# Four transformer layers on one core: expert weights by SyncE's direct DMAs, and GpSimd's scatters and fetches one by one behind a TensorE product

## The reference

```
x = x + xattn0(ln(x), ctx);  x = x + ln(x) @ sign(weight).T
x = x + xattn1(ln(x), ctx)
h = ln(x)                                   # 2048 tokens
score = softmax(h @ gate_w.T);  w, e = top_k(score, 2)
x = x + sum_k w_k * (silu(h @ w_gate[e_k]) * (h @ w_up[e_k])) @ w_down[e_k] + shared(h)
x = x + xattn2(ctx, ln(x), mask);  x = x + ternary_ffn(ln(x))
x = x + xattn3(ln(x), ctx);        x = x + three_lora_blocks(ln(x))
```

## Time and profile before

| | us |
|---|---|
| median of 3 runs (1206.04 to 1211.15) | 1206.27 |
| the profiled execution | 1206.1 |
| its span, first to last instruction | 1204.3 |
| TensorE busy | 1059.1 |
| VectorE busy | 935.3 |
| ScalarE busy | 825.4 |
| GpSimd busy | 549.8 |

### The profile page before, as it was taken

How to read it: one execution, slowest core, us unless ns; L and a number is a source line. 1 busy time by engine, 2 the same in 40 slices (tenths; PEclk the granted TensorE clock), 3 DMA queues, 4 the chain that set the end, 5 groups by cost and what they waited for, 6 DMA issues and landing times.

```text
span 1204.3 us, 25939 instructions
## 1 busy us (share of the span) xinstructions
PE 1059.1 (88%) x8349; PEld 787.6 (65%) x8406; DVE 935.3 (78%) x3207; ACT 825.4 (69%) x1560; POOL 549.8 (46%) x1089
## 2 busy tenths in 40 slices
PE   5899999987999988799899997689998999988876
PEld 4677777775878866567677774347575665656654
DVE  1888888777555679897777698899989989898633
ACT  4677756655665646557557767459989798998963
POOL 5233255665444466468744426124424432324235
PEclk8999999999999999999999999889999999999989
DMA  5675542325577542513387762132212222121000
GB/s 175 200 242 185 173 113 67 98 68 149 174 225 195 171 137 71 149 36 106 113 250 231 230 200 79 53 90 67 73 35 66 80 62 80 54 63 54 10 10 18
DMA packets 98356, 140.01 MB, mean 116 GB/s; under 512 B 12336, under 2 KB 79792, under 8 KB 98224
## 3 DMA queue, kind: packets, MB, share of 16 engines
q1 hardware_dynamic: 90192, 105.58, 29.7%
q0 software_dynamic: 8032, 32.78, 9.0%
HBM read 65.43 MB, written 22.54 MB: 73 GB/s over the span
## 4 chain that ended last, share of the span: by engine, by line
PE 47%; DVE 21%; ACT 12%; issue 9%; DMA 4%; POOL 3%; another core or an unknown queue 2%; SPq 1%; DVEq 0%; ACTq 0%; POOLq 0%
PE ps L1513 10%; PE ps L1634 5%; PE ps L1533 4%; PE ps L1551 4%; PE ps L1506 4%; PE ps L1726 4%; ACT probs L1942 3%; DVE neg_max L2197 3%; DVE ps L2193 3%; PE ps L1520 3%; PE ps L1733 2%; DVE bn L2074 2%; DMA w<-in_expert,w_row 2%; ACT q_st L1957 2%
## 5 line engine op out<-in xcount | busy, mean ns | idle before, releaser
L1942 ACT ACTIVATE probs<-ps 128x384 f32<-128x384 f32 (+1 forms) x512 | 264.0, 545 | 62.4 <-PE ps L1554 28.8
L1533 PE MATMUL ps<-k_st,q_st 96*128 96x256 bf16 (+1 forms) x1024 | 173.7, 261 | 26.0 <-DVE neg_max L2197 10.8
L1551 PE MATMUL ps<-q_st,k_st 104*128 104x256 bf16 (+1 forms) x1024 | 179.0, 261 | 14.8 <-ACT probs L1942 6.6
L2197 DVE TENSOR_REDUCE neg_max<-ps 128x2 f32<-128x512 f32 x256 | 168.2, 680 | 12.2 <-PE ps L1536 6.4
L1957 ACT ACTIVATE q_st<-ps 8x1024 bf16<-8x1024 f32 x128 | 130.2, 1017 | 48.9 <-PE ps L1616 39.0
L2193 DVE CUSTOM_DVE_ANT_0 ps<-ps,diag_s 128x128 f32<-128x128 f32 (+1 forms) x384 | 123.2, 358 | 30.9 <-PE ps L1533 21.9
L2514 POOL TENSOR_SCALAR var_eps<-mv 128x2 f32<-128x2 f32 (+1 forms) x115 | 27.5, 239 | 253.2 <-DVE mv L2077 242.3
L1533 PEld LDWEIGHTS ps<-k_st,q_st 96*128 96x128 bf16 x1024 | 86.6, 98 | 75.5 <-DVE neg_max L2197 21.2
L1551 PEld LDWEIGHTS ps<-q_st,k_st 104*128 104x128 bf16 x1024 | 89.8, 98 | 61.2 <-issue 17.9
L1634 PE MATMUL ps<-probs,v 128*32 128x256 f32 (+1 forms) x2048 | 125.4, 363 | 4.3 <-ACT probs L1942 2.6
L2532 POOL CAST parts<-qf 128x512 bf16<-128x512 f32 x64 | 39.8, 622 | 150.1 <-DVE qf L2099 67.9
(11 more groups left out here) (271 smaller groups left out, 2584.5 us busy)
## 6 DMA issues: line engine op xcount, KB each, us to landing
k_st<-parts SPq DMA_DIRECT2D x192, 128.0 KB
q_st<-parts SPq DMA_DIRECT2D x192, 128.0 KB
x_rows<-wo SPq DMA_DIRECT2D x10, 768.0 KB, 6.5
ctx_t<-in_ctx_t SPq DMA_DIRECT2D x16, 256.0 KB, 3.9
ring<-x_rows SPq DMA_DIRECT2D x31, 128.0 KB
y_rows<-ring SPq DMA_DIRECT2D x31, 128.0 KB
xn_t<-x_rows SPq DMA_DIRECT2D x31, 128.0 KB
y_rows<-vec SPq DMA_DIRECT2D x31, 128.0 KB
```

The lines of the kernel that those rows point to most:

```text
L1533: last = mm(t[:, c0:c0 + n], head(q_st, r, h, KROWS, j * P, P), head(k_st, r, h, KROWS, 0, n), start=j == 0 or L != 2, stop=L != 2, skip_g ...
L1551: last = mm(t[:, j * S:j * S + n], head(k_st, r, h, KALL, j * P, P), head(q_st, r, h, KALL, skip, n), start=j == 0 or L == 3, stop=L == 3, ...
L1942: nc.scalar.activation(probs[:, (hg % 2) * HPG + h4, 0:width], tile_of(key)[:, 0:width], ACT.Exp, scale=SCALE).then_inc(*tile_drained(key))
L2197: V.tensor_reduce(neg_max[:, hg, h4, :], tile_of(key).rearrange("p (j t) -> p j t", j=SJ), AX.X, ALU.max, negate=True).then_inc(*tile_drai ...
```

## The change

1. `gather` moves from GpSimd's stream to SyncE's. SyncE waits for the same semaphores, reads the expert's row number from `w_row` into a register, and issues one direct DMA from there.
2. `scatter` and `fetch` are cut into four steps each, one for each indirect DMA, with a time of its own in `AT`.
3. Ahead of each of these 64 DMAs GpSimd waits for the last score product of TensorE that the plan puts before the DMA (`wait_score`).
4. All of `AT` is written anew. Its last step stands at 1117.9 us, where it stood at 1120.5.

```diff
-    yield
-    part.scatter(b)
+    for a in range(SJ):
+        for k in range(TOP_K):
+            yield
+            part.scatter(b, a, k)
...
-    yield
-    part.fetch(b)
+    for a in range(SJ):
+        for k in range(TOP_K):
+            yield
+            part.fetch(b, a, k)
     yield
     part.merge(b)
...
+            def wait_score():
+
+                n = sum(10 * clock[0] > t for t in AT[0])
+                if n:
+                    L, b = ORDER[(n - 1) // H]
+                    wait_filled(pool, ("s", L, b, *divmod((n - 1) % H, HPG)))
...
-                def gather(i):
-                    wait_drained(pool, ("tile_e", i // GT))
-                    if i >= RING:
-                        wait_filled(pool, ("gd", i - RING))
-                    G.indirect_dma_start(expert[:, i % RING, :], None, expert_d,
-                                         bass.IndirectOffsetOnAxis(ap=w_row[:, i:i + 1], axis=0)).then_inc(*w_tile_in[i % RING].step(i))
...
+                    wait_score()
+                    G.indirect_dma_start(x_rows[b // NB], bass.IndirectOffsetOnAxis(ap=dest[:, b * SJ + a, k:k + 1], axis=0),
+                                         xn[:, NORMED["l1f"], a, :], None).then_inc(*scattered.step((b, a, k)))
...
+                    wait_score()
+                    G.indirect_dma_start(y_in(b, n), None, y_rows[g],
+                                         bass.IndirectOffsetOnAxis(ap=dest[:, T, k:k + 1], axis=0)).then_inc(*y_back[n % RING].step(n))
...
+                def gather(i):
+                    wait_drained(sp, ("tile_e", i // GT))
+                    if i >= RING:
+                        wait_filled(sp, ("gd", i - RING))
+                    row = sp.value_load(w_row[0:1, i:i + 1], min_val=0, max_val=(E - 1) * P)
+                    sp.dma_start(expert[:, i % RING, :], expert_d[bass.ds(row, P), :]).then_inc(*w_tile_in[i % RING].step(i))
```

More of the change, by code:

```diff
@@ L2661, in allotted, with scatter, fetch @@
                     done(G.tensor_tensor(owner[:, b // NB, :], owner[:, b // NB, :], less[:, 1, :], ALU.add), "owner")
-                def scatter(b):
-                    pool.wait_ge(*place.at(("dest", b)))
-                    pool.wait_ge(*ln_done.at(("l1f", b, SJ - 1)))
-                    if b == 0:
-                        pool.wait_ge(*filling.at(11))
-                    for a in range(SJ):
-                        for k in range(TOP_K):
-                            G.indirect_dma_start(x_rows[b // NB], bass.IndirectOffsetOnAxis(ap=dest[:, b * SJ + a, k:k + 1], axis=0),
-                                                 xn[:, NORMED["l1f"], a, :], None).then_inc(*scattered.step((b, a, k)))
-                def gather(i):
-                    wait_drained(pool, ("tile_e", i // GT))
-                    if i >= RING:
-                        wait_filled(pool, ("gd", i - RING))
-                    G.indirect_dma_start(expert[:, i % RING, :], None, expert_d,
-                                         bass.IndirectOffsetOnAxis(ap=w_row[:, i:i + 1], axis=0)).then_inc(*w_tile_in[i % RING].step(i))
-                def fetch(b):
-                    g = b // NB
-                    if b % NB == 0:
+                def scatter(b, a, k):
+                    if a == k == 0:
+                        pool.wait_ge(*place.at(("dest", b)))
+                        pool.wait_ge(*ln_done.at(("l1f", b, SJ - 1)))
+                        if b == 0:
+                            pool.wait_ge(*filling.at(11))
+                    wait_score()
+                    G.indirect_dma_start(x_rows[b // NB], bass.IndirectOffsetOnAxis(ap=dest[:, b * SJ + a, k:k + 1], axis=0),
+                                         xn[:, NORMED["l1f"], a, :], None).then_inc(*scattered.step((b, a, k)))
+                def fetch(b, a, k):
+                    g, T = b // NB, b * SJ + a
+                    n = T * TOP_K + k
+                    if b % NB:
+                        pool.wait_ge(*merged.at((b - 1, a, k)))
+                    elif a == k == 0:
                         wait_filled(pool, ("gt", (g + 1) * GT - 1))
@@ L2686, in fetch @@
                             pool.wait_ge(*y_out[i % RING].at(i))
-                    for a in range(SJ):
-                        for k in range(TOP_K):
-                            T = b * SJ + a
-                            n = T * TOP_K + k
-                            if b % NB:
-                                pool.wait_ge(*merged.at((b - 1, a, k)))
-                            G.indirect_dma_start(y_in(b, n), None, y_rows[g],
-                                                 bass.IndirectOffsetOnAxis(ap=dest[:, T, k:k + 1], axis=0)).then_inc(*y_back[n % RING].step(n))
+                    wait_score()
+                    G.indirect_dma_start(y_in(b, n), None, y_rows[g],
+                                         bass.IndirectOffsetOnAxis(ap=dest[:, T, k:k + 1], axis=0)).then_inc(*y_back[n % RING].step(n))
                 def block_power(n, b):
```

## The result

| | before, us | after, us | ratio |
|---|---|---|---|
| medians of 13 and 13 runs on one chip | 1208.83 | 1198.55 | 0.9906 [0.9885, 0.9927] |
| once more on another chip, 20 and 12 runs | 1207.64 | 1198.82 | 0.9928 [0.9901, 0.9955] |

What follows compares the result with a forecast made beforehand. No engine was full; TensorE's work (busy 88%) plus its waits was taken as the time. 1206.1 - 13 - 1.5 + 0 + 4 - 1.3 = 1194.3, 0.2 more by the median, taken as 1194 us; range 1177 to 1207.

Steps and rivals of the forecast that it cites:

- The reading of the stalls: During bursts of indirect DMAs on GpSimd, news of finished TensorE products reaches other engines only afterwards; 29 us of stalls.
- Rival 2: Stalls come from the transfers' own traffic or chance, not GpSimd, and stay; 1207.5 us, chance 0.07.
- Rival 1: Waits on GpSimd don't break the bursts; only what the gathers prolonged goes; 1202 us, chance 0.16.
- 1% or less: Predicted share of the changed kernel's chain under "another core or an unknown queue", 2% before.
- 1 us at most: Predicted longest joint restart delay of ScalarE and VectorE right behind a burst in the changed profile.
- -13 us for the stalls: At 16 bursts of scatters and fetches: 19 us of stall go, 0.7 of it counts, between -5 and -24.
- The added waits on GpSimd, 0: 64 waits for scores on GpSimd cost nothing, being hidden by slack; at worst 13.9 us.
- The slack that I named: GpSimd's 242.3 us in 58 waits, 4.2 us each, said to hide a wait of one or two us.
- GpSimd relieved, -1.5: 62 gathers leave GpSimd, so `power` and splits come sooner; a tenth of ScalarE's 13.9 us wait for `shift`.
- SyncE loaded, +4 us: Loads, stores and stacks queue behind gathers of 1.3 us each on SyncE; between 0 and 9 us.
- The new table, -1.3 ± 5: The rewritten order of steps ends 2.6 us earlier in the plan; half counted, ±5 us either way.
- Rivals 3 and 4: SyncE bounds the expert stretches, 1220 us, chance 0.10; all stalls count, single gathers hold signals too, 1178 us, chance 0.15.

Runs made afterwards that it cites:

- r_after: The changed kernel, unchanged, run again on chip C beside the kernel before: 1198.82 us, ratio 0.9928.
- e2: The changed kernel with its own table and split steps but without its waits for score products, on chip A: 1199.53 us, ratio 0.9933 to before.
- e9: The kernel before with split steps and waits ahead of scatters, fetches and also gathers, gathers on GpSimd, on chip B: 1194.05 us, ratio 1.0022.
- e10: The same kernel as e9, run on chip D: 1193.82 us, ratio 1.0042 to before.
- e1: The kernel before with only the gathers moved to SyncE, old table, no waits, on chip A: 1214.84 us, ratio 1.0067.
- e4: The changed kernel with the old table, scatters and fetches split 1.3 us apart, on chip A: 1210.91 us, ratio 1.0028 to before.
- e3: The kernel before with only split steps and waits ahead of scatters and fetches, gathers on GpSimd, on chip A: 1197.41 us, ratio 0.9924.
- r_waits_only: The same kernel as e3, run again on chip C: 1196.62 us, ratio 0.9912 to before.
- e8: The changed kernel, but waiting for TensorE's last product of any kind instead of the last score product, on chip B: 1204.21 us, ratio 1.0118 to before.
- e6: As e3, but with an extra `power` on GpSimd ahead of each DMA in place of the wait, on chip B: 1221.51 us, ratio 1.0258 to before.

## Why the prediction was right, point by point

**The reading of the stalls** held on the chips where signals are held. The waits alone took 9.2 and 11.0 us off, and in the pair above the products ended on time and only the news was late. Rival 2 (not of GpSimd's making) falls there, though on B and D there are no stalls to take away. Rival 1 (the waits don't break the bursts) falls too: the chain's share went to 0%, against "1% or less", and the scatters of batch 3 stand up to 2.2 us apart. Of the changed kernel's bursts four are whole, where the prediction counted two; 31 of 48 gaps are still 0.3 us. One mark was missed: a piece behind a burst was to be 1 us at most, and one is 1.48 (2.08 in r_after).

**-13 us for the stalls**: 9.2 and 11.0 were measured for the waits alone, with the burst of gathers left whole. In the full change the terms don't add up. On chip A the waits are worth 9.2 us with the gathers on GpSimd and 3.9 us (1214.84 to 1210.91) with them on SyncE, where the long burst is already shorter. In the new plan they are worth 0 to 3 us (e2). For the waits alone the term was right in kind and 2 to 4 us too large; as a part of the full change it was 9 us or more too large.

The prediction has no term for the clock, and a stall costs more than its length. In before TensorE stood 4.63 us up to 289.42, and the granted clock, 1.00 until then, was 0.52 and 0.63 in the next four us (column before the last two), between the two levels of 1.2 and 2.4 GHz; the 16 value products at 290.03 took 1.51 us, where those at 280.97 took 0.86. After had 1.00 from 270 to 295 us. The rows of before, then of after:

```profile
290.00:292.00 2.00, 2.00 (x21) 1.08 (x21) 1.63 (x7) 0.83 (x2) 0.22 (x1) 0.52 0.44 157
292.00:294.00 2.00, 2.00 (x17) 1.71 (x16) 1.76 (x10) 1.16 (x3) 1.69 (x4) 0.63 0.00 0
```

```profile
290.00:295.00 5.00, 5.00 (x45) 4.54 (x42) 4.46 (x19) 4.50 (x12) 2.75 (x6) 1.00 0.69 186
```

As an estimate from these rows, the slower clock takes 2 x 0.48 + 2 x 0.37 = 1.7 us of TensorE's work there. Over the whole run it doesn't show: the mean clock of after isn't higher than that of before.

**The added waits on GpSimd, 0**: about right for the waits. GpSimd's scatters by line, then ScalarE's waits, of after:

```profile
L2681 POOL DMA_INDIRECT x_rows<-xn,dest x32 | 32.7, 1021 | 20.2 <-PE ps L1557 9.9 <-issue 7.3 <-PE ps L1560 1.8
```

```profile
ACT xn L1896 <- POOL shift L2523: 12.0, 15, 1.8
...
ACT o_raw L1953 <- remote: 6.6, 3, 2.8
```

GpSimd stood 20.2 us ahead of them (9.7), 11.7 of that for TensorE, and ScalarE's wait for `shift` is 12.0 us (13.9); its longest wait without a releaser is 2.8 us, where it was 5.38. On B and D, where there is nothing to win, e9 and e10 cost 0.2 and 0.4%, 3 to 5 us. The slack that I named isn't for everything: 0.75 us more of work at each of the 64 places cost 31.

**GpSimd relieved, -1.5**: no run has it alone; ScalarE's wait for `shift` fell by 1.9 us, the most that it can be at this place.

**SyncE loaded, +4 us**: the step that was mis-sized most. It measured +8.2 (e1, what the shorter bursts gave already taken off) and +13.5 (e4 against e3). The price of one gather was too high, and what it does to the others too low. SyncE's rows between 270 and 420 us in after, by line:

```profile
L2818 SPq TENSOR_LOAD <-w_row x31: 262/275/686, 275.4 to 390.8; - x31
L2818 SPq FUSED_REGOPS  x31: 152/152/184, 276.1 to 391.1; - x31
```

```profile
L2819 SPq DMA_DIRECT2D w<-in_expert x31: 13/348/362, 276.6 to 391.5; - x31
...
DMA to landing us min/median/max: 3.2/4.1/5.3
```

The last gather begins at 390.8 and its issue ends at 391.82 (391.47 and 0.35 us): 1.0 us in all, where I took 1.3. The Trainium skill, DMA: Bandwidth & Descriptors, section "Latency and other measured facts", puts a register load at 0.6 us or more; the load and its arithmetic are 0.43 us here (0.275 and 0.152 in the median), so that figure is too high for this trace, while my estimate of 0.9 us for a gather from it came out 0.1 too low. The cost lay elsewhere. A direct DMA of weights stands in SyncE's order beside six stacks, and lands late: the 5.7 us at 356 us. I had reckoned with waits behind a gather, not with a gather's own landing. The base was misread too: with the row for `ring<-x_rows` TensorE's waits were 7.9 us in 8 waits, not 6.8 in 7.

**The new table, -1.3 ± 5**: 12 to 15 us with the gathers on SyncE (15.3 from e1 to e2, on one chip), outside my ±5, because I took it as a plan by itself. Its worth, as far as TensorE's waits for DMAs tell, is that it sets the gathers where SyncE's other DMAs leave them room. TensorE's waits for the three sorts were to rise from 6.8 to about 11 us and are 5.8. This error and the last have opposite signs: 4 - 1.3 was predicted for the two together, and the difference measured between after and the waits alone is +2.2 us on chip C and -2.2 us by the ratios of the first runs on two chips, nothing that shows. So the sum held although two terms didn't, and the third is smaller in the full change than alone. By the runs on chip A (those of after are on others) the full change is made up of +8.2 us (gathers), -15.3 (table) and 0 to -3 (waits), or, in the other order, of -9.2 (waits), +13.5 (gathers) and -12 to -15 (table); predicted were -13, +2.5 with GpSimd's relief, and -1.3. The reading of the stalls was right, as the waits alone show. That the time came within 5 us of the sum is in good part luck.

**Rivals 3 and 4**: SyncE isn't full (TensorE waited for a stack once, 0.2 us), and 1178 was never near (by the prediction's own terms that sum is 1177.5: -1.5 + 4 - 1.3 is 1.2, not 2). What the slower side of my chances missed is the chip: nothing in one trace could tell that 17.7 to 22 us of it would not be there on others.

**The rule against my reading.** The Trainium skill, SBUF — State Buffer, section "SBUF: two separate sides", says that at the ports of SBUF TensorE and ScalarE never wait on anyone. The pair above fits it better than the prediction allowed: TensorE's products took 1.07 us on both chips, and ScalarE's row names no instruction that kept it. What the rule doesn't give is the conclusion that ScalarE can't stop; on chip C it did, for 6.07 us.

**Still open**: (1) the changed kernel itself wasn't run on a chip of the second kind. It took 1198.6 and 1198.8 us on two of the first kind; kernels with the old table and waits took 1197 on A and C (e3, r_waits_only) and 1194 on B and D (e9, e10, whose gathers wait too). If after too stands there up to 3 us under its 1198.6, it is 0.5 to 0.8% slower than before (1195.6 to 1198.6 against 1190). e8, which differs from after in what its DMAs wait for, took 1204.2, 1.2% more than before. That is an estimate from these medians, not a run. (2) Spacing or the wait itself: e6 ran on a chip without stalls. (3) Whether the changed kernel needs its waits, and whether e3's gain would come without them on the same chip by another order. (4) By what path a signal is held.

## What to carry to other kernels

A chain piece without a releaser in a program on one core is worth the look: find what all such pieces have in common, then test by adding only a wait. Where the order of operations stays the same, lay the two traces side by side and read where the time is won. When work moves to another engine's queue, count what stands beside each DMA in that queue and when it lands, not only the time of issuing, and place it and its neighbours in the order together: the move cost 8 to 14 us in the old order and nothing that shows in the new. Measure a change of 1% on more than one chip; here the kernel before differs by 1.3 to 1.7% between chips, more than the whole gain. Waits alone are the simplest version that has the gain (1196.6 to 1197.4 us where signals are held); where they aren't held, the kernels nearest to it (e9, e10) took 3 to 5 us more than before.

## What the runs showed of the hardware

- On chips A and C, and on that of the result, four to seven indirect DMAs of GpSimd in a row, 1.0 us each and 0.3 us apart, kept finished products of TensorE from the other engines, 4.03 us in the pair; on chip D the same burst kept it for 0.13 us.
- The kernel before takes 1206 to 1209 us on the former and 1189 to 1191 on B and D. The granted clock explains a small part: its median over the runs of before is 0.969 on A and C and 0.973 on B and D, and the runs of after, from 1189.44 us at 0.980 to 1199.21 at 0.966, give 0.7 us for 0.001 of clock, so, as an estimate, some 3 of the 17 us.
- After TensorE had stood 4.63 us in before, its granted clock was 0.52, then 0.63, in the four us that followed; in after, without that stall, it was 1.00 from 270 to 295 us.
- A gather of 384 KB by SyncE takes 1.0 us of its queue and lands after 3.2 to 5.3 us in after; among stacks it took 5.7 us in e1.
